# Stage one reordered, half of the routing inside it, and the slots taken batches 0 to 3 first, in a one-core two-layer block

## The reference, cut to what matters

```python
x = L0_attn_x                                   # [8 batches, 512 tokens, 128]
xn = layernorm(x)
x = x + linear_attention(xn) + mx_ffn(xn)       # 16 heads of 8, rope, rmsnorm of q and k; FP6 grid, blocks of 32
xn = layernorm(x)
# attention of layer 1 runs over the 8 batches, for each token and head by itself:
attn = softmax(q @ k.T / sqrt(8)) @ v           # 8 x 8 for each of 512 tokens x 16 heads
x = x + attn @ out_w.T + out_b + moe(xn)
# moe: sigmoid gate of 16 experts in 4 groups; best 2 groups by their best pair; best 4 experts;
# routed = sum over experts of w * (silu(x @ w1) * (x @ w3)) @ w2, plus one shared expert
```

## Time and profile before

| | |
|---|---|
| three runs, us | 403.55, 407.75, 407.75; median 407.75 |
| the profiled execution, us | 408.82, its span 405.9 |
| mean granted clock of TensorE | 0.937 of full speed |
| stage one, from the first instruction to the copy of the last l1 tile | 0 to 172.2 us |
| routing until the first `hidden` has ended | 172.2 to 210.1 us |
| slots 0 to 3, up to the last `hidden` of slot 3 | 210.1 to 302.7 us |
| the rest | 302.7 to 405.9 us |
| single instructions of ScalarE and VectorE: sigmoid 0.42, copy of `combT` 0.60, silu 0.60; sum of p 1.07, `residual` 0.68, us | |
| busy shares: TensorE, VectorE, GpSimd, ScalarE | 80%, 84%, 58%, 46% |

### The profile page before, as it was taken

The page is one execution under the profiler, slowest core; times in us unless marked ns, Lnnn a source line. Parts: engine busy times, 40 slices in busy tenths (PEclk is TensorE's granted clock), DMA queues, the critical chain, the costliest instruction groups (busy, mean ns, idle before and its releaser), DMA issues.

```text
span 405.9 us, 5042 instructions
## 1 busy us (share of the span) xinstructions
PE 325.6 (80%) x1455; PEld 238.8 (59%) x1455; DVE 342.2 (84%) x846; ACT 187.4 (46%) x502; POOL 236.5 (58%) x157
## 2 busy tenths in 40 slices
PE   0179889889889875706029999999999999999995
PEld 0047667868768675704016666666666666666662
DVE  4875889797876765599999899999999999999891
ACT  0553567876866735703022352625326262442521
POOL 9053584473563521094075959778695987867450
PEclk9996989999999988776759999999999999999999
DMA  7810000110110112120000000000010000000000
GB/s 184 263 23 1 2 0 2 53 52 2 52 53 1 53 52 97 66 52 1 0 1 0 2 1 26 2 26 0 1 28 0 26 2 27 0 2 26 0 26 27
DMA packets 13248, 12.49 MB, mean 31 GB/s; under 512 B 1549, under 2 KB 9925, under 8 KB 13221
## 3 DMA queue, kind: packets, MB, share of 16 engines
q1 hardware_dynamic: 10944, 10.10, 7.9%
q0 software_dynamic: 736, 0.95, 1.1%
q10 hardware_dynamic: 1540, 1.12, 1.0%
HBM read 5.88 MB, written 2.10 MB: 20 GB/s over the span
## 4 chain that ended last, share of the span: by engine, by line
PE 53%; DVE 25%; issue 7%; POOL 6%; ACT 5%; DMA 1%; ACTq 1%; POOLq 0%; DVEq 0%
PE Q L838 18%; PE VK L838 15%; PE T L838 9%; PE ND L838 7%; POOL prod_qk L778 3%; POOL prod_pv L788 2%; DVE rope_a L1248 2%; DVE rope_b L1250 2%; PE T L834 2%; PE Q L834 2%; DMA headmask<-in_c_headsel 1%; DVE attn L1280 1%; DVE chosen L1414 1%; DVE scr L1344 1%; DVE den L1277 1%
## 5 line engine op out<-in xcount | busy, mean ns | idle before, releaser
L788 POOL TENSOR_TENSOR prod_pv<-prob,qkv 128x1024 f32<-128x1024 f32 x32 | 69.6, 2212 | 45.0 <-DVE att L1361 24.2
L689 ACT ACTIVATE sg<-Q 128x512 f32<-128x512 f32 x72 | 43.1, 598 | 97.7 <-PE Q L838 94.9
L778 POOL TENSOR_TENSOR prod_qk<-qkv 128x1024 f32<-128x1024 f32 x32 | 75.9, 2397 | 16.7 <-DVE scr L1344 16.7
L838 PE MATMUL VK<-hid,w 128*128 128x512 f32 x144 | 74.5, 599 | 0.0
L838 PE MATMUL Q<-xT_hi,w_hi 128*128 128x512 f32 x72 | 52.3, 727 | 0.7 <-ACT combT L675 0.7
L1444 DVE TENSOR_TENSOR sgc<-ND,sg 128x512 f32<-128x512 f32 x64 | 43.7, 683 | 6.7 <-PE ND L838 4.6
L1457 DVE TENSOR_TENSOR hid<-T,sgc 128x512 f32<-128x512 f32 x64 | 43.6, 682 | 0.3
L838 PE MATMUL T<-xT_hi,w_hi 128*128 128x512 f32 x72 | 28.8, 401 | 17.1 <-DVE hid L1457 17.1
L838 PE MATMUL Q<-bias,ones 128*128 128x400 f32 (+1 forms) x64 | 29.7, 464 | 14.3 <-DVE xTs_lo L1299 9.2
L1344 DVE TENSOR_REDUCE scr<-prod_qk 128x128 f32<-128x1024 f32 x32 | 38.5, 1208 | 0.0
L1361 DVE TENSOR_REDUCE att<-prod_pv 128x128 f32<-128x1024 f32 x32 | 38.3, 1198 | 0.0
(11 more groups left out here) (189 smaller groups left out, 795.9 us busy)
## 6 DMA issues: line engine op xcount, KB each, us to landing
xT_hi<-xTs_hi SPq DMA_DIRECT2D x8, 256.0 KB, 2.3
xT_lo<-xTs_lo SPq DMA_DIRECT2D x8, 256.0 KB, 2.3
out_x<-fin SPq DMA_DIRECT2D x8, 256.0 KB, 2.3
x<-in_x SPq DMA_DIRECT2D x2, 256.0 KB, 4.8
wraw<-in_w1T SPq DMA_DIRECT2D x1, 512.0 KB, 9.7
w<-in_w2T SPq DMA_DIRECT2D x1, 512.0 KB, 6.0
wraw<-in_w3T ACTq DMA_DIRECT2D x1, 512.0 KB, 3.2
sel<-in_c_sel POOLq DMA_DIRECT2D x4, 128.0 KB, 2.8
```

What stands on the lines that cost most here:

```text
L689: act.activation(sg[:, side(half, s), :], QB[side(half, s)][:, :], ACT.Silu).then_inc(sg_ready, 1)
L778: pool.tensor_tensor(prod_qk[:, t % 2], bc(qkv2[:, TH * half + t, j, 0:D], 1, NB), qkv2[:, :, j, D:2 * D], ALU.mult).then_inc(qk_prod, 1)
L788: pool.tensor_tensor(prod_pv[:, t % 2].rearrange("p (h e) b -> p b h e", e=HD), bc(prob[:, t], 3, HD), qkv2[:, :, j, 2 * D:QKV].rearrange( ...
L838: return pe.matmul(o, lhsT, rhs, start=start, stop=stop)
```

## The change: what it does

**Stage one.** The four `step` functions are reordered. TensorE does the transposes of the rotated q and the value product ahead of the q, k, v tiles of the next batch, and the output product ahead of the l1 tiles; the q transposes move from bank T1 to T0. VectorE does `head_blocks`, `plus_ffn` ahead of `mx_scales`, `stats(0)` after the first rope tile, and `rope_tile(3)` between `ln_values` and `rms_values`. ScalarE copies `xnT` ahead of the root, and squares of tiles 2 and 3 move behind the output squares.

**Weights.** Both `low_part`s move from VectorE to GpSimd, `sel` is zeroed and loaded there in step 9, and the load of `w3` moves from ScalarE's queue to SP's.

**Routing.** `route(h)` is cut into seven parts. For half 0 they run in steps 9 (`route_pairs`, `route_ranks`), 10 (`route_allowed`) and 11 (`route_top`, `route_chosen`), the last two after the pipeline; its sigmoid runs in step 9, with an unused square root behind it. For half 1 they run between slices of slots 0 to 3. Slot `n` becomes tile `n % 4` of batches 0 to 3 (`n` below 4) or 4 to 7, so half 1 is wanted only from slot 4.

**Slots.** The first product's scores are reduced in slot 0's own slices; the exponential comes after slice 5, 4, 2 in slots 0, 1, 2 and after 1 from there on. `scr` and `prob` are laid out with the batch innermost.

```diff
@@ ScalarE, step
+                run(i, 1, xnT_evac)
                 norms_rooted(i)
+                if at(i, STEPS - 3):
+                    sigmoid(0)
                 weights_of_step(i)
-                run(i, 1, xnT_evac)
+                run_next(i, 5, l1_tile(2))
                 run(i, 2, xdT_evac)
...
+                if at(i, STEPS - 3):
+                    act.activation(vu_n[:, 0, :], vu_n[:, 0, :], ACT.Sqrt)
...
+                run(i, 2, out_squares)
+                run(i, 4, l1_tile(0))
+                run(i, 1, qkv_tile(2))
                 run(i, 1, qkv_tile(3))
-                run(i, 4, l1_tile(0))
-                run(i, 2, out_squares)
                 run(i, 4, l1_tile(1))
@@ GpSimd, step
                 run(i, 3, residual)
+                if i == STEPS - 3:
+                    low_part(w1_lo[:, :], wraw[:, :], w1_hi[:, :], w1_hi_ready, w1_ready)
+                    sel_padded()
+                if i == STEPS - 2:
+                    low_part(w3_lo[:, :], wraw[:, :], w3_hi[:, :], w3_hi_ready, w3_ready)
@@ TensorE, step
                 run(i, 1, xn_transposes)
+                run_next(i, 5, l1_tile(2))
                 run(i, 3, ffn_product)
                 run(i, 2, xd_transposes)
-                run_next(i, 5, l1_tile(2))
+                run(i, 2, qf_transposes)
+                run(i, 2, value_product)
+                run_next(i, 5, l1_tile(3))
                 run(i, 1, qkv_tile(0))
-                run(i, 2, qf_transposes)
-                run_next(i, 5, l1_tile(3))
+                run(i, 2, numerators)
                 run(i, 1, qkv_tile(1))
-                run(i, 2, value_product)
                 run(i, 4, xn2_transposes(i))
-                run(i, 2, numerators)
+                run(i, 2, attn_transposes(i))
                 run(i, 1, qkv_tile(2))
+                run(i, 2, output_product)
+                run(i, 4, l1_tile(0))
                 run(i, 1, qkv_tile(3))
@@ VectorE, step
+                run(i, 2, head_blocks)
+                run(i, 3, plus_ffn)
+                if at(i, STEPS - 3):
+                    route_pairs(0)
+                if at(i, STEPS - 2):
+                    route_allowed(0)
                 run(i, 1, mx_scales)
...
+                run(i, 1, rope_tile(0))
+                run(i, -1, stats(0, stats1_ready))
+                run(i, 2, attention)
                 if at(i, STEPS - 3):
+                    route_ranks(0)
                 run(i, 1, rope_tile(1))
                 run(i, 1, mx_magic)
+                run(i, 3, stats(1, stats2_ready))
+                run(i, 4, xn2T_lo_part)
                 run(i, 1, rope_tile(2))
                 if before_last(i):
                     ln_values(i)
+                run(i, 1, rope_tile(3))
+                if before_last(i):
                     rms_values(i)
@@ VectorE, layout: scores, and the maximum of them
-                V.tensor_reduce(scr[:, half, t], prod_qk[:, t % 2]...
+                V.tensor_reduce(scr[:, n % 2, t].rearrange("p h b -> p b h"), prod_qk[:, t % 2]...
-                V.tensor_reduce(smax[:, :, :], scr[:, half].rearrange("p t b h -> p t h b"), AX_X, ALU.max)\
+                V.tensor_reduce(smax[:, :, :], scr[:, n % 2], AX_X, ALU.max)\
@@ VectorE, after the pipeline
-            route(0)
-            scores(0, 0, 0)
-            scores(0, 1, 0)
-            route(1)
-            scores(0, 2, 0)
-            scores(0, 3, 0)
+            route_weights(0)
+            route_parts(0)
@@ VectorE, slots
+            def route_later(n, s):
+                if (n, s) == (0, 7):
+                    route_pairs(1)
+                if (n, s) == (0, 8):
+                    route_ranks(1)
+                if (n, s) == (1, 1):
+                    route_allowed(1)
+                if (n, s) == (1, 8):
+                    route_top(1)
+                if (n, s) == (2, 0):
+                    route_chosen(1)
+                if (n, s) == (2, 5):
+                    route_weights(1)
+                if (n, s) == (3, 1):
+                    route_parts(1)
...
+            def first_slot(s):
+                if s < TH:
+                    scores(0, s)
+                if s == 4:
+                    less_max(0)
+                if s == 5:
+                    scores(1, 0)
+                    sum_of_p(0)
+                if s == 6:
+                    over_sum(0)
+                    dve.wait_ge(xT_kept, 32 * NB)
+                    values(0, 0)
+                if s == 7:
+                    scores(1, 1)
+                    values(0, 1)
+                if s == 8:
+                    values(0, 2)
...
                 for s in range(NS):
+                    weighted(n, s, side(n, s))
+                    ...
+                    route_later(n, s)
+                    hidden(n, s, side(n, s))
@@ TensorE, before and in slot 0
-            comb_transposes(0)
-            pe.wait_ge(combT_ready, 1)
-            pe.wait_ge(ld_sel, 16 * NJ)
+            pe.wait_ge(l1_kept, NT)
...
+                    if n == 0 and s == 0:
+                        comb_transposes(0)
@@ GpSimd, products in the slots
-                        bc(prob[:, t], 3, HD),
+                        bc(prob[:, t].rearrange("p h b -> p b h"), 3, HD),
```

More of the change, by code:

```diff
@@ L276, in build @@
         early.close()
[L279 to L299, removed]
+        sel = sb("sel", [P, NJ, NS - 1, P], F32R)
+        sc = sb("sc", [P, NT, NE])
+        pairs = sb("pairs", [P, NH * NG, NPAIR])
+        gs = sb("gs", [P, NH * NG])
+        cmp_gt = sb("cmp_gt", [P, NH, NG, NG])
+        cmp_eq = sb("cmp_eq", [P, NH, NG, NG])
+        rank = sb("rank", [P, NH * NG])
+        allowed = sb("allowed", [P, NH * NG])
+        minus1 = sb("minus1", [P, NH * NG])
+        sa = sb("sa", [P, NH, NE])
+        masked = sb("masked", [P, NH, NE])
+        top = sb("top", [P, NH, 8])
+        chosen = sb("chosen", [P, NH, NE])
+        wsel = sb("wsel", [P, NH, NE])
+        wsum = sb("wsum", [P, 3, NH])
+        comb2 = wraw[:, 0:NT * 2 * NE].rearrange("p (t e) -> p t e", e=2 * NE)
         prod_pv = sb("prod_pv", [P, 2, D, NB])
@@ L406, in slots, with side, follow @@
             for n in range(NSLOT):
[L407 to L424, removed]
+                slot(n, n % NJ, n // NJ)
+        COMB_SLOT, COMB_SLICE = NJ - 1, 6
+        EXP_SLICE = [5, 4, 2] + [1] * (NSLOT - 3)
+        def side(n, s):
+            return (n + s) % 2
+        def follow(n):
+            return None if n == NSLOT - 1 else ((n + 1) % NJ, (n + 1) // NJ)
         def blocks(t):
@@ L479, in exp_of, with run @@
         def exp_of(act):
-            def run(n, half):
+            def run(n):
                 act.wait_ge(s_sub, n + 1)
@@ L661, in last_step @@
                 xn2T_hi_evac(NB - 1)
-                sigmoid(0)
                 for j in range(NJ):
@@ L813, in slot @@
             def slot(n, j, half):
-                nxt = follow(n, j, half)
+                nxt = follow(n)
                 def next_qk(t):
@@ L1308, in step @@
                 if at(i, STEPS - 1):
-                    low_part(w3_lo[:, :], wraw[:, :], w3_hi[:, :], w3_hi_ready, w3_ready)
+                    route_top(0)
+                    route_chosen(0)
                 run(i, 2, features)
@@ L1335, in step, with scores @@
                     vu_sum()
-            def scores(n, t, half):
+            def scores(n, t):
                 u = TH * n + t
@@ new lines, in second_slot @@
+            def second_slot(s):
+                if s == 0:
+                    values(0, 3)
+                if s in (1, 2):
+                    scores(1, 1 + s)
+                if s == 3:
+                    less_max(1)
+                if s == 4:
+                    residual(0)
+                    scores(2, 0)
+                    sum_of_p(1)
+                if s == 5:
+                    over_sum(1)
+                if s >= 5:
+                    values(1, s - 5)
+                if s == 7:
+                    scores(2, 1)
@@ new lines, in third_slot @@
+            def third_slot(s):
+                if s in (0, 1):
+                    scores(2, 2 + s)
+                if s == 1:
+                    less_max(2)
+                if s in (2, 3):
+                    scores(3, s - 2)
+                if s == 3:
+                    sum_of_p(2)
+                if s == 4:
+                    residual(1)
+                    over_sum(2)
+                if 4 <= s < 4 + TH:
+                    values(2, s - 4)
+                if s in (7, 8):
+                    scores(3, s - 5)
@@ new lines, in later_slot @@
+            def later_slot(n, s):
+                more = follow(n) is not None
+                if s == 0:
+                    less_max(n)
+                if s == 2:
+                    sum_of_p(n)
+                if s in (1, 2, 7, 8) and more:
+                    scores(n + 1, {1: 0, 2: 1, 7: 2, 8: 3}[s])
+                if s == 3:
+                    over_sum(n)
```

(4 more changed lines are left out.)

248 lines of the change are left out of this document (126 added, 122 removed).

## The result

| | before | after |
|---|---|---|
| median, us | 407.75 (403.55 to 408.03, 4 runs) | 416.52 (415.2 to 417.1, 4 runs) |
| ratio | | 1.0248, 95% interval 1.0200 to 1.0296 |
| profiled execution, its span, us | 408.82, 405.9 | 415.2, 413.4 |
| 1. to the end of the last l1 copy | 172.2 | 175.2 |
| 2. from there to the end of the first `hidden` | 37.9 | 6.6 |

The kernel is 2.5% slower by the ratio of the runs on record (the two medians, divided, give 1.0215). Each line of the stretches is a difference of the starts (plus lengths) of single instructions, as in the earlier trace rows; the four differences, +3.0, -31.3, +27.3 and +8.6, make up the 7.5 us between the spans.

What follows compares the result with a forecast made beforehand. Bounds: a VectorE-TensorE loop in stage one, VectorE almost alone in routing, TensorE in slots, VectorE having 0.7 us to spare. Sum 2 - 31.1 + 24.8 - 2.8 = -7.1 us, median 400.7 us; forecast 396 to 404, range 387 to 413.

Steps and rivals of the forecast that it cites:

- Parts 1 and 2: Stage one's steps and its end: gains spent on new waits, +2 us together, range -4 to +7.
- rival B: Stage one gets shorter: a step some 0.9 us less, -6 in six steps, 395 us; chance 0.12.
- part 2: End of stage one: VectorE's small operations wait for GpSimd's added work, such as zeroing `sel`; +2 us, 0 to +5.
- Part 3: Routing off the path: 6.8 us from last l1 copy to first `hidden`, against 37.9; -31.1 us.
- Part 4: Slots 0 to 3: VectorE becomes the bound with added routing, scores and waits for GpSimd products; +24.8 us, +11 to +28.
- Part 5: From slot 4 on: as before, 103.2 us, less TensorE's two slices ahead and some `normalise` waits; -2.8 us.
- C: Slots: GpSimd reads `prob` more slowly in the new layout, `prod_pv` 2.21 to 3.4 us; slower, 414 us; chance 0.10.
- A: Slots 0 to 3: routing meets no products, waits fall from 12.4 us to some 3; 391 us; chance 0.17.
- D: Whole kernel: nothing much moves; stage one's step gains 0.7 us of waits, routing meets every product; 407 us; chance 0.16.

Runs made afterwards that it cites:

- e3_both_orders: Changed kernel with the exponential ahead of `yT` and scores and sum of p ahead of `weighted(2)`, both from slot 3 on; ratio 1.0105 to the kernel before.
- e5: Changed kernel, exponential ahead of `yT` from slot 4, scores and sum of p ahead of `weighted(2)`, `sel` zeroed after the last `rms_values`; 1.0003 of the kernel before.
- e9_two_and_chosen: Changed kernel, exponential ahead of `yT` from slot 4, scores and sum of p ahead of `weighted(2)`, `route_chosen(1)` ahead of `weighted(2,0)`; 0.9879 of the kernel before.
- e10_layout_alone: Kernel before the change with only the new layout of `scr` and `prob`; ratio 0.9871 to the kernel before.
- e4_sel_late: Changed kernel with the zeroing and loading of `sel` moved from step 9 to step 10, behind the split of `w3`; ratio 1.0413 to the kernel before.

## Why the prediction was wrong

It said -7.1 us and a range to 413; measured was +8.8 between the medians, +7.5 between the spans.

*Parts 1 and 2, +2 with a range to +7*: +3.0. A full step was 15.58 us (roots below), not 16.1, so rival B was right in a third of its size; other steps took more than that back: one early step 16.48 us for 14.73 (from the root at 60.76), step 9 17.86 where before had 16.12, step 10 8.33 for 6.95.

```profile
108.39 0.24 ACT L601 ACTIVATE root<-root 128x20 f32<-128x20 f32 x1
...
123.97 0.24 ACT L601 ACTIVATE root<-root 128x20 f32<-128x20 f32 x1
```

The mechanism of part 2, `rms_values` under the zeroing, is there (3.50 us), but it was not shown to be on the path alone: it and a late rise of TensorE's clock cover each other.

*Part 3, -31.1*: -31.3. The instruction list from the last copy to the first `hidden` gave 6.8 us, 6.6 were measured.

*Part 4, +24.8*: +27.3. The size is near, but the mechanism only in part, so the near size is in part luck: the waits were put too high and idle times left out. The routing met four products (1, 0, 1, 2 and 0 in its pairs, ranks, allowed, weights and parts) and was held for some 7.5 us, where the sum had 5.4 products and 12.4 us; leaving it out gave 10.3 us rather than 24.1. What was missing from the sum were idle times of VectorE, 7.6 us with the routing in place and 16.2 without it, among them 2.99 us in slot 2, where TensorE waits for `normalise(1)`, since the last `values` of slot 1 stand at slice 8, and 1.85 us for the silu in slot 3. The prediction took VectorE as always busy and added work and waits; the part of the work that fills such idle times costs nothing, and the idle times that no work fills cost what they are.

*Part 5, -2.8: the step that failed.* It began with "As before". Measured: +8.6. That is 11.4 of the 14.6 us by which the span lies over its sum of 398.8; part 4 is 2.5 of them, parts 1 and 2 are 1.0. Slots from 4 on were not as before: two edits in the order, the exponential behind `yT` and `weighted(2)` ahead of what needs no silu, were in the diff, and the text of the change even names the second; neither was costed. Taking both back moved these slots from 26.7 to 23.8 us and the rest from 111.8 to 101.9 (e3_both_orders; 101.6 in e5), where 100.4 had been forecast. The working for it was at hand: VectorE had 0.7 us to spare in a slot, and the exponential with its two table loads is 3.2 us of ScalarE on the way to a silu.

*The layout* was put at 0.7 us a slot on VectorE and counted in full only in slots 0 to 3; part 5 gave it about 1 us. By itself it takes 4.8 us off the span of the kernel before (405.9 to 401.1). That TensorE was "busy" for the whole of a slot had made the prediction take its 24.1 us as a floor.

*The rivals.* C is refuted: `prod_pv` reads the new layout in 2.20 us (2.21 in the earlier trace rows). A's claim that the routing meets no products is refuted too (7.5 us held, where A had some 3); D, that nothing much moves, underrated the loss. The mechanism that decided was none of them.

What the whole change is worth once mended: the new order of the slots with its faults taken out (e9_two_and_chosen, 0.9879) is no quicker than the old order with the new layout (e10_layout_alone, 0.9871) on the same chip; the intervals lie over each other. In these two profiles it saves 29.1 us of exposed routing (6.6 for 35.6) and gives back 24.1 in slots 0 to 3 and 3.2 in stage one. The 2.3 us that are left between these two spans are no gain: the profiles are of the fastest of six executions of e9 and the slowest of six of e10, and the medians are 401.6 and 401.9 us. As the order stands, the layout is all that the change brings.

## What to carry to other kernels

For every instruction that a change swaps with a neighbour, write down what each side waits for, even where the section is "as before": an instruction put behind one that waits inherits that wait, and here two such swaps cost 2.9 us in each slot from slot 4 on. A bound engine's busy share near 100% is no floor when the engine is pipelined; look for its waits in the list as well. And test the small, local part of a large change alone, first: it may hold the whole gain.

## What the runs showed of the hardware

A zeroing by GpSimd (128x4096, 3.51 us) holds VectorE's `rms_values`, 12 columns wide, for all of it (3.50 us; after):

```profile
150.69 2.65 POOL L761 TENSOR_TENSOR w_lo<-wraw,w_hi 128x1152 fp32r<-128x1152 f32 x1 [4.94 <-ACT w_hi L520]
151.71 5.10 DVE L1118 TENSOR_SCALAR root<-mv 128x8 f32<-128x8 f32 x1
153.27 3.51 POOL L766 MEMSET sel<- 128x4096 f32 x1
153.32 3.50 DVE L1124 TENSOR_SCALAR root<-ss 128x12 f32<-128x12 f32 x1
```

That agrees with the Trainium skill, "SBUF — State Buffer", section "Who interferes with whom". The instruction ahead of it, 8 columns wide, shows one thing more: started at 151.71 under GpSimd's split of `w1` (over at 153.3), it did not get through between split and zeroing and was over only at 156.81, with the zeroing. In e4_sel_late it was the same (3.90 us, from 162.23, under the split of `w3` and the zeroing). The copy with conversion in e3_both_orders (2.15 us for 0.29) was held too.

Which way such meetings fall turns on tenths of a microsecond: one subtraction took 2.69 us in the kernel before, where it started 0.20 us behind a product, and 0.71 in e10_layout_alone, where it started 0.13 us ahead of one; there the product took 2.83 us for 2.34.

TensorE's clock rose from 1.2 to 2.4 GHz at different times in executions of the same code, with TensorE busy for all of the windows around it (2.00 of 2.00 at a granted 0.50 and 0.63 above); in step 9 of the two kernels without the zeroing there that is 17.88 - 16.42 = 1.5 us.
